# Scores and attention three units further ahead of the projections, and every group written out, in a masked attention layer

## What is computed

```python
q = heads(x @ Wq + bq)
k = heads(x @ Wk + bk)
v = heads(x @ Wv + bv)
scores = jnp.einsum('bhqd,bhkd->bhqk', q, k) * scale
scores = jnp.where(mask[:, None] == 0, -jnp.inf, scores)
attn = jax.nn.softmax(scores, axis=-1)
out = jnp.einsum('bhqk,bhkd->bhqd', attn, v)
out = out.transpose(0, 2, 1, 3).reshape(b, s, D_MODEL)
return _layernorm(x + out @ Wo + bo)
```

## Time and profile before

| | |
|---|---|
| time, median of 3 runs | 911.61 us (910.68 to 912.45) |
| the profiled execution's own time | 910.95 us |
| its span, first to last instruction | 909.2 us |
| busy: PE, DVE, ACT, POOL | 96%, 89%, 76%, 30% of the span |
| prologue, to the first score product | 0 to 29.5 us |
| group 0 on PE | 29.83 to 54.15 us |
| groups 1 to 29 on PE | 54.15 to 836.57 us |
| mean share of the full TensorE clock | 0.986 |

### The profile page before, as it was taken

The page is one execution under the profiler, slowest core; times in us unless marked ns, Lnnn a source line. Parts: engine busy times, 40 slices in busy tenths (PEclk is TensorE's granted clock), DMA queues, the critical chain, the costliest instruction groups (busy, mean ns, idle before and its releaser), DMA issues.

```text
span 909.2 us, 34909 instructions
## 1 busy us (share of the span) xinstructions
PE 870.0 (96%) x11784; PEld 606.9 (67%) x11784; DVE 809.6 (89%) x3449; ACT 689.1 (76%) x1745; POOL 273.0 (30%) x386
## 2 busy tenths in 40 slices
PE   6989999999999999999999999999999999999954
PEld 4666667777666777666777666777766677766632
DVE  5789899989899999999999999998989999999984
ACT  5787788777787887777877778877778788777761
POOL 0122233332323333323333223333232333322222
PEclk9999999999999999999999999999999999999967
DMA  8277887876678877678877677787667887667863
GB/s 301 60 148 135 140 175 172 179 160 151 129 166 179 176 161 148 149 143 176 179 167 169 125 151 168 172 178 167 142 137 159 179 177 161 149 148 149 149 140 93
DMA packets 362287, 143.33 MB, mean 158 GB/s; under 512 B 340752, under 2 KB 344848, under 8 KB 361872
## 3 DMA queue, kind: packets, MB, share of 16 engines
q1 hardware_dynamic: 362256, 142.93, 73.3%
HBM read 42.21 MB, written 16.78 MB: 65 GB/s over the span
## 4 chain that ended last, share of the span: by engine, by line
PE 71%; DVE 21%; issue 4%; DMA 2%; DVEq 1%; ACT 0%; SPq 0%; POOL 0%; POOLq 0%; ACTq 0%
PE proj_ps L610 57%; PE score_ps L610 7%; PE av_ps L610 6%; DVE masked L497 6%; DVE p_pair L484 5%; DVE stats L526 3%; DVE y L523 3%; DVE qT_lo L477 1%; DVE v_parts L470 1%; DMA pT<-p_pair 1%; DVE minus_max L497 1%; DVE inv_sum L506 1%; DMA w_land<-weights 1%; DVE attn L511 0%; DMA aT<-a_pair 0%
## 5 line engine op out<-in xcount | busy, mean ns | idle before, releaser
L412 ACT ACTIVATE probs<-masked,minus_max 128x128 f32<-128x128 f32 x1024 | 326.9, 391 | 170.3 <-DVE minus_max L497 165.9
L497 DVE CUSTOM_DVE_ANT_0 masked<-score_ps,mask 128x128 f32<-128x128 f32 x1024 | 236.9, 287 | 48.2 <-PE score_ps L610 29.8
L484 DVE SCALAR_TENSOR_TENSOR p_pair<-probs,p_pair 128x512 f16<-128x512 f32 x256 | 196.6, 768 | 1.3 <-ACT p_pair L422 1.1
L422 ACT ACTIVATE p_pair<-probs 128x512 f16<-128x512 f32 x256 | 161.3, 630 | 13.3
L610 PE MATMUL proj_ps<-wo_hi,aT 128*128 128x512 f16 x512 | 166.4, 387 | 2.4 <-DMA aT<-a_pair 1.5
L230 POOL TENSOR_TENSOR xT_lo<-xT_raw,xT_hi 128x512 f16<-128x512 f32 x60 | 70.0, 1166 | 309.3 <-ACT xT_hi L375 309.3
L610 PE MATMUL proj_ps<-xT_hi,wq_hi 128*128 128x256 f16 x512 | 141.3, 276 | 11.3 <-DVE wq_lo L578 7.9
L610 PE MATMUL proj_ps<-xT_hi,wk_hi 128*128 128x256 f16 x512 | 140.3, 274 | 2.6 <-DVE qT_lo L477 2.4
L610 PE MATMUL proj_ps<-xT_lo,wq_hi 128*128 128x256 f16 x512 | 140.7, 275 | 0.0
L610 PE MATMUL proj_ps<-xT_hi,wq_lo 128*128 128x256 f16 x512 | 140.7, 275 | 0.0
L610 PE MATMUL proj_ps<-xT_hi,wk_lo 128*128 128x256 f16 x512 | 139.7, 273 | 0.0
(11 more groups left out here) (58 smaller groups left out, 1523.0 us busy)
## 6 DMA issues: line engine op xcount, KB each, us to landing
xT_raw<-x_cols SPq DMA_DIRECT2D x32, 512.0 KB, 4.3
x_in<-x_rows SPq DMA_DIRECT2D x32, 512.0 KB, 5.0
out<-y SPq DMA_DIRECT2D x64, 256.0 KB, 2.6
adj_in<-adj SPq DMA_DIRECT2D x32, 128.0 KB, 2.4
pT<-p_pair SPq DMA_TRANSPOSE x256, 3.1
w_land<-weights SPq DMA_DIRECT2D x2, 1024.0 KB, 7.7
w_land<-weights SPq DMA_DIRECT2D x4, 256.0 KB, 5.5
x_res<-weights SPq DMA_DIRECT2D x1, 1024.0 KB, 9.6
```

The source lines that it names most:

```text
L412: ins = act.activation(probs[s % 2][:, j * S:(j + 1) * S], masked[s % 2][:, j], ACT.Exp, bias=minus_max[s % 2][:, j:j + 1], scale=-1.0)
L422: act.activation(p_pair[s % NT][:, 0:HW], probs[s % 2][:], ACT.Copy, scale=P_UP).then_inc(p_hi_done, 1)
L484: dve.scalar_tensor_tensor(out=p_pair[s % NT][:, HW:2 * HW], in0=probs[s % 2][:], scalar=P_UP, in1=p_pair[s % NT][:, 0:HW], op0=ALU.mult, ...
L497: ins = dve.tensor_tensor_reduce(masked[s % 2][:, j], score_ps[j][:, s % HC], mask[par][:, s // KC], -EXP_SCALE, 3.0e38, ALU.add, ALU.min, ...
```

## The change

Line numbers below are those of the changed kernel where order rows say L5xx or L6xx with another number than before; the functions are the same.

- `scored(g, s, par)` says which units' scores PE makes in step s: the one four ahead (AHEAD = 4) instead of one ahead. In steps 0 to 3 of group 0 it is units 1, then 2 and 3, 4 and 5, 6 and 7 (FIRST). In the last group only steps 0 to 3 have scores.
- `attend` takes the unit four back from the one scored, so unit s in step s, instead of s - 3.
- `softmaxed(g, s, par)` gives DVE, ACT and SP the unit that PE scored one step earlier.
- Y0 and Y1 change places in TASKS: Y1 of the previous group in step 5, Y0 of the **same** group in step 7.
- On ACT the high part of the attention result moves from steps 0 and 4 to 1 and 5, and its low part on DVE from steps 2 and 4 to 2 (graph 1 of the group before) and 5 (graph 0 of this group, ahead of the low part of V0). SP turns it in step 5 ahead of that step's probabilities.
- The second `high_part_x` and `low_part_x` move one step earlier, the mask from step 5 to 3, stores and the normalizations swap graphs and steps.
- The loop is gone: all 32 groups are written out.

```diff
-    TASKS = ((Q, 0), (Q, 1), (K, 0), (K, 1), (V, 0), (Y, 0), (V, 1), (Y, 1))
-    LAG = 3
+    TASKS = ((Q, 0), (Q, 1), (K, 0), (K, 1), (V, 0), (Y, 1), (V, 1), (Y, 0))
+    AHEAD = 4
+
+    FIRST = ((1,), (2, 3), (4, 5), (6, 7))
...
+    def scored(g, s, par):
+
+        if isinstance(g, int) and g == 0 and s < AHEAD:
+            return [(0, t, 0) for t in FIRST[s]]
+        if s < SLOTS - AHEAD:
+            return [(g, s + AHEAD, par)]
+        return [(g + 1, s + AHEAD - SLOTS, 1 - par)] if has_next(g) else []
+
+    def softmaxed(g, s, par):
+
+        if s > 0:
+            return scored(g, s - 1, par)
+        return [(0, 0, 0)] if isinstance(g, int) and g == 0 else [(g, AHEAD - 1, par)]
...
-    def all_groups(eng, group):
-        group(0, 0, 0)
-        group(1, 1, 0)
-        with eng.Fori(1, NG // 2 - 1) as k:
-            group(2 * k, 0, k)
-            group(2 * k + 1, 1, k)
-        group(NG - 2, 0, NG // 2 - 1)
-        group(NG - 1, 1, NG // 2 - 1)
+    def all_groups(group):
+        for g in range(NG):
+            group(g, g % 2, g // 2)
...
-                    before, slot = back(g, s, 1)
-                    if exists(before):
-                        turn_probs(before, slot)
+                    if s == 5 and has_next(g):
+                        turn_attn(g, 0)
+                    for unit_g, t, _ in softmaxed(g, s, par):
+                        before, slot = back(unit_g, t, 1)
+                        if exists(before):
+                            turn_probs(before, slot)
...
-                    if s in (2, 4) and at_least(g, 1):
-                        turn_attn(g - 1, s // 4)
-                    if s in (0, 2) and at_least(g, 2):
-                        store(g - 2, s // 2)
+                    if s == 1 and at_least(g, 2):
+                        store(g - 2, 1)
+                    if s == 2 and at_least(g, 1):
+                        turn_attn(g - 1, 1)
+                        store(g - 1, 0)
...
-                    if s in (0, 4) and at_least(g, 1):
-                        high_part_attn(g - 1, s // 4)
+                    if s == 1 and at_least(g, 1):
+                        high_part_attn(g - 1, 1)
+                    if s == 5:
+                        high_part_attn(g, 0)
...
-                    exponentials(g, s)
-                    high_part_probs(g, s)
-                    if s in (2, 5) and has_x_next2(g):
-                        high_part_x(g + 2, (s - 2) // 3, par)
+                    for unit_g, t, _ in softmaxed(g, s, par):
+                        exponentials(unit_g, t)
+                        high_part_probs(unit_g, t)
+                    if s in (2, 4) and has_x_next2(g):
+                        high_part_x(g + 2, (s - 2) // 2, par)
...
-                    masked_max(g, s, par)
-                    before, slot = back(g, s, 1)
-                    if exists(before):
-                        low_part_probs(before, slot)
-                    if s > 0 and TASKS[s - 1][0] != Y and has_next(g):
-                        low_part_bank(g + 1, *TASKS[s - 1], nxt)
-                    if s in (2, 4) and at_least(g, 1):
-                        low_part_attn(g - 1, s // 4)
-                    before, slot = back(g, s, LAG + 1)
-                    if exists(before):
-                        head_norm(before, slot)
-                    if s == 0 and at_least(g, 2):
-                        y_and_moments(g - 2, 1, par)
-                    if s == 6 and at_least(g, 1):
+                    for i, (unit_g, t, unit_par) in enumerate(softmaxed(g, s, par)):
+                        masked_max(unit_g, t, unit_par)
+                        before, slot = back(unit_g, t, 1)
+                        if exists(before):
+                            low_part_probs(before, slot)
+                        if i == 0:
+                            if s == 5:
+                                low_part_attn(g, 0)
+                            if s > 0 and TASKS[s - 1][0] != Y and has_next(g):
+                                low_part_bank(g + 1, *TASKS[s - 1], nxt)
+                            if s == 2 and at_least(g, 1):
+                                low_part_attn(g - 1, 1)
+                        before, slot = back(unit_g, t, AHEAD)
+                        if exists(before):
+                            head_norm(before, slot)
+                    if s == 0 and at_least(g, 1):
                         y_and_moments(g - 1, 0, nxt)
+                    if s == 6 and at_least(g, 1) and has_next(g):
+                        y_and_moments(g - 1, 1, nxt)
...
-                    if s == 5 and has_next(g):
+                    if s == 3 and has_next(g):
                         make_mask(g + 1, nxt, k + par)
...
-                    before, slot = back(g, s, LAG)
-                    if not has_next(g) and s < SLOTS - 1:
-                        scores(g, s + 1, par)
-                    if exists(before):
-                        attend(before, slot, par if s >= LAG else nxt)
-                    if has_next(g):
-                        if s < SLOTS - 1:
-                            scores(g, s + 1, par)
-                        else:
-                            scores(g + 1, 0, nxt)
+                    if not has_next(g):
+                        for unit_g, t, unit_par in scored(g, s, par):
+                            scores(unit_g, t, unit_par)
+                        attend(g, s, par)
+                        continue
+                    for unit_g, t, unit_par in scored(g, s, par):
+                        before, slot = back(unit_g, t, AHEAD)
+                        if exists(before):
+                            attend(before, slot, par)
+                        scores(unit_g, t, unit_par)
```

More of the change, by code:

```diff
@@ L308, in _ @@
             load_x(1, 1)
-            all_groups(sp, group)
+            all_groups(group)
             turn_probs(LAST, SLOTS - 1)
-            store(LAST - 1, 0)
             turn_attn(LAST, 0)
@@ L345, in group @@
                 for s in range(SLOTS):
-                    if s == 1 and at_least(g, 2):
-                        normalize(g - 2, 1)
+                    if s == 1 and at_least(g, 1):
+                        normalize(g - 1, 0)
                     if s == 2:
@@ L353, in group @@
                         residual(g, 1, par, k)
-                    if s in (3, 6) and has_x_next2(g):
-                        low_part_x(pool, g + 2, (s - 3) // 3, par)
+                    if s in (3, 5) and has_x_next2(g):
+                        low_part_x(pool, g + 2, (s - 3) // 2, par)
                     if s == 7 and at_least(g, 1):
-                        normalize(g - 1, 0)
+                        normalize(g - 1, 1)
             pool.memset(minus_half[:], -0.5).then_inc(const_made, 1)
@@ L361, in _ @@
             pool.wait_ge(const_made, 2)
-            all_groups(pool, group)
-            normalize(LAST - 1, 1)
+            all_groups(group)
             normalize(LAST, 0)
@@ L454, in _ @@
                     high_part_bank(0, V, 1, 0, True)
-            all_groups(act, group)
-            high_part_attn(LAST, 0)
+            all_groups(group)
             high_part_attn(LAST, 1)
@@ L594, in _ @@
                     low_part_bank(0, V, 1, 0, True)
-            all_groups(dve, group)
+            all_groups(group)
             low_part_probs(LAST, SLOTS - 1)
@@ L662, in step_bank @@
                 if kind == Y:
-                    if not at_least(g, 1):
+                    of = g if i == 0 else g - 1
+                    if not exists(of) or not has_next(of):
                         return
-                    if i == 1:
-                        pe.wait_ge(y_summed, batch(g - 1, 0) + 1)
+                    if i == 0 and at_least(g, 1):
+                        pe.wait_ge(y_summed, batch(g - 1, 1) + 1)
                     elif has_next(g):
@@ L669, in step_bank @@
                     else:
-                        pe.wait_ge(y_summed, batch(g - 2, 1) + 1)
-                    y_bank(g - 1, i)
+                        pe.wait_ge(y_summed, batch(g - 1, 0) + 1)
+                    y_bank(of, i)
                     return
@@ L683, in step_bank @@
                     pe.wait_ge(split_out, split_no(g, V, 1) + 1)
-                elif at_least(g, 2):
-                    pe.wait_ge(y_summed, batch(g - 2, 1) + 1)
                 else:
-                    pe.wait_ge(split_out, split_no(g, K, 1) + 1)
+                    pe.wait_ge(y_summed, batch(g - 1, 0) + 1)
                 split_bank(g + 1, kind, i, nxt)
@@ L748, in _ @@
             scores(0, 0, 0)
-            all_groups(pe, group)
-            attend(LAST, SLOTS - 3, LAST % 2)
-            attend(LAST, SLOTS - 2, LAST % 2)
-            attend(LAST, SLOTS - 1, LAST % 2)
+            all_groups(group)
             y_bank(LAST, 0)
```

## The result

| | before | changed |
|---|---|---|
| median of 6 runs each, us | 911.05 | 916.97 |
| lowest to highest | 910.00 to 912.45 | 914.79 to 918.57 |
| profiled execution, own time | 910.95 | 918.14 |

A forecast was written before the change was run, and what follows sets the result against it. PE was taken to bound the middle, softmax on DVE and ACT the end. From a 909.2 us span, -7.5 + 5.8 + 2.5 + 4.8 - 11.3 - 0.1 = -5.8 gave 903.4, as run median 906 us; range 902 to 910.

The forecast's parts named there:

- (c): Y0 of the same group in step 7 needs aT turned in time; 0.5 us to spare, cost nothing.
- aT of Y0 lands late: Rival: turns take longer where loads are under way; 0.2 us over the margin would give 912 us; chance 0.06.
- No loop: Groups 1 to 29 without the loop's returns: 0.26 us less for each of 29 groups, -7.5 us.
- Straight code costs nothing: Fetching written-out code in the groups put at nothing, since group 29 in straight code shows no cost.
- (b): V1 in step 6 waits for V0's low part, delayed by POOL's low_part_x: 0.20 us in 29 groups, +5.8 us.
- (a): Scores of the next group's unit 0 in step 4 need K1's low part; 0.36 us to spare, cost nothing.
- The rival with 0.14: K1's low part becomes the bound in step 4: scores wait up to 0.4 us per group, 917.6 us; chance 0.14.
- The head: Group 0: second scores and V1 wait, +2.5 us beyond 4.8 us of work moved ahead; bounds 0 and 4.
- The end: From unit 3's scores in the last group on: 34.8 us instead of 46.1, -11.3 us; bounds 33.5 and 37.

The follow-up runs named there:

- e3: Changed kernel with PE's program alone back in a loop, the other four engines' programs written out: 915.61 us, ratio 1.0027 to the kernel before.
- e5: Changed kernel with the low part of the attention result ahead of that of the probabilities on DVE in step 5: 914.18 us, ratio 1.0025 to the kernel before.
- e7: Changed kernel with the edits of e5 and e6 together: 906.84 us, ratio 0.9948 to the kernel before.
- e1: Kernel before with all 32 groups written out and nothing else changed: 904.34 us, ratio 0.9910 to the kernel before.
- e6: Changed kernel with the splits of the next x (ACT's high part, POOL's low part) back in their old steps: 911.98 us, ratio 0.9999 to the kernel before.
- e4: Changed kernel with 47 filler products in group 0 where PE waited: 915.89 us, ratio 1.0042 to the kernel before.
- e9: e7 with 88 filler products in PE's waits of the last group: 907.67 us, ratio 0.9946 to the kernel before.
- e2: Changed kernel with the loop over groups 2 to 29 put back for all engines: 975.97 us, ratio 1.0695 to the kernel before.
- e10: e7 with the first unit of steps 1 to 3 in group 0 placed between the projection bank's halves: 906.21 us, ratio 0.9941 to the kernel before.

## Why the prediction was wrong

It put the span at 903.4 us; the profiled execution had 916.4. The 13.0 us are 8.9 in groups 1 to 29 (780.7 forecast, 789.6 measured), 3.5 in group 0 (31.6, 35.1), 1.6 from group 30 to the end, and -1.0 in the prologue, which is scatter: it varies by 2 us between kernels that share it. In groups 1 to 29 the 8.9 are 10.4 of waits for aT, where the sum had none, less 1.5 by which V1's waits fell short of theirs.

**The step that failed is (c)**, "0.5 us to spare ... Nothing." The margin was real, 0.4 us in undisturbed groups (aT lands at 23.0 us of the group, Y0 wants it at 23.4), but it was measured with the loop's DMA traffic. The same change that shortened the distance from a_pair to Y0 wrote the groups out, and so multiplied the packets of PE's code by five. A turn that meets one 1.1 to 3.0 us after its issue takes 4.3 to 5.0 instead of 3.3 us: 8.4 of the 10.4 us of waits. e3 (packets away, waits 3.0), e5 and e7 (issue earlier, waits 6.7 and 4.2) and e1 (packets there, a later use of aT, waits 1.6) show both halves to be needed. The rival "aT of Y0 lands late" named the place, but for another cause (loads) and with a chance of 0.06. The trace of before could have told: of its 64 turns of aT five meet such a packet, in groups 1 to 3, where code is still fetched, and four of these take 4.7 to 6.8 us, while none of the 58 that meet no code at all takes over 4.5. The prediction took 3.1 us instead, which is the median of the probabilities' turns. What a turn and the packet contend for, the traces don't show; that stays open.

**"No loop", -7.5.** Right in kind: e1 gives -6.3 us in the middle, of which 1.6 went to aT even there. "Straight code costs nothing" was right of the engines' own streams and wrong of the queues beside them. The Trainium skill ("Runtime: NRT & Kernel Launch", Instruction fetch mechanics) calls the crossing of a block mostly hidden. For PE itself the traces agree, its groups run at 26.70 us; but a transpose under way at the same time takes up to 1.7 us more.

**(b) V1's wait, +5.8.** Mechanism right, size a little off: 0.13 us in a typical group, 4.3 in all. p_pair ends 0.54 us after POOL, as in the earlier trace rows, but POOL starts 0.13 us sooner than the working has it, so p_pair takes 1.04 us in most groups instead of 1.15. e6 removed it by moving POOL's operation.

**(a) K1's low part, nothing.** Right: no group of the changed kernel shows scores that wait for kT_lo. The rival with 0.14 did not occur.

**The head, +2.5 beyond the work moved.** Measured +5.9, outside its bound of 4. The waits were foreseen; that they bring the clock down was not (2.1 us, e4). Without that it would be 3.8, inside the bound.

**The end, 34.8 us.** 36.5 measured, within the bounds of 33.5 and 37. Most of the difference is clock and the wait of Y1 of group 30 for aT (0.57 us); e9 shows that a full clock would have given back only 0.9.

**What the lead itself is worth.** e7 against e1, both written out: group 0 +8.0, the end -9.4, the middle +3.4. As whole kernels 906.84 against 904.34 us, with overlapping intervals. So even with V1's wait gone and the waits for aT at 4.2 us, working three units ahead moves idle time from the end to the start and buys nothing that can be measured. The two ends alone would leave it 1.4 us; no kernel here has them without the loss in the middle. The only gain in this change that is clear of noise is the loop's.

## What to carry to other kernels

Where an edit takes slack from a transfer, measure the transfer's duration under the traffic that the edited program will have, code fetch included: unrolling feeds a queue, and a margin of 0.5 us on a 3.3 us turn is none if 8 such turns in 29 take 4.3 to 5.0. Take a change that bundles a simple gain with a deep reordering apart first; here writing the groups out was alone worth 0.9%, and the reordering took it all and more. A lead at the end is paid for at the start, waits, clock and all, so both ends belong in one sum.

## What was not expected of the hardware

- A return of the loop cost DVE 0.57 us in the kernel before and 3.5 us in e2, with the same 3449 counted instructions on DVE but code packets in each pass.
- A single 16 KB packet of code beside a transpose (1.1 to 3.0 us after its issue) cost it 1.0 to 1.7 us, though these packets are 0.7% of the DMA engines' time.
- The same instructions met different clocks. e7 and e9 do the same work up to the last group. PE in V1's bank of group 0, in e7 and in e9, behind the same wait:

```profile
55.36 0.38 PE L629 MATMUL proj_ps<-wv_lo,xT_hi 128*128 128x512 f16 x1
```

```profile
56.61 0.63 PE L629 MATMUL proj_ps<-wv_lo,xT_hi 128*128 128x512 f16 x1
```

It is worth 2.6 us for group 0 (32.3 and 34.9), more than several of the edits above. In runs of e10 (902.81 to 910.11 us) the mean clock was 0.989 in the fastest and 0.984 in the slowest. What decides which clock an execution meets is not shown.
